# A 16 x 256 token RWKV and mixture-of-experts layer: earlier loads and norms, 22 idle products, a first table in PSUM, a tail on two queues

## What is computed

```python
x = x + attn(_layernorm(x), ...)
x = x + moe(_layernorm(x), ...)

# attn
xn = _ln(x, ln1_g, ln1_b); xp = _shift(xn)
k = (xn * mix_k + xp * (1.0 - mix_k)) @ Wk          # v and r likewise
r = sigmoid(...)
# per feature, along the tokens: a = ew*a + exp(k)*v;  b = ew*b + exp(k);  wkv = a / (b + 1e-8)
x = x + r * wkv @ Wo
yn = _ln(x, ln2_g, ln2_b); yp = _shift(yn)
kk = square(relu((0.5 * yn + 0.5 * yp) @ Wfk))
return x + sigmoid(yn @ Wfr) * (kk @ Wfv)

# moe: 8 experts, the best 2 of each token, hidden size 256
total_probs = softmax of the top 2 of x @ gate_w, at their experts
hidden = silu(h1) * h2                               # h1, h2 = x @ w12 of each expert
y = sum over experts of total_probs * (hidden @ w3)
```

## Time and profile before

| | |
|---|---|
| Runs | 330.14, 330.01, 329.98 us; median 330.01 |
| Profiled execution | 332.63 us, span 330.8 us, mean granted clock 0.92 |
| PE busy | 260.2 us (79%) |
| DVE busy | 241.2 us (73%) |
| POOL busy | 212.0 us (64%) |
| ACT busy | 196.4 us (59%) |
| Moved | 29.23 MB, mean 88 GB/s |

### The profile page before, as it was taken

One profiled execution on the slowest core, in us unless ns is written; L12 is line 12 of the kernel. 1 busy time (PEld: TensorE's weight loads), 2 busy tenths in 40 slices (PEclk: granted clock), 3 DMA queues, 4 the chain that ended last, 5 costly groups with the idle time before them and its releaser, 6 DMA issues.

```text
span 330.8 us, 6269 instructions
## 1 busy us (share of the span) xinstructions
PE 260.2 (79%) x1684; PEld 206.3 (62%) x1684; DVE 241.2 (73%) x735; ACT 196.4 (59%) x412; POOL 212.0 (64%) x225
## 2 busy tenths in 40 slices
PE   0684869999979999794796899379998799999300
PEld 0231347485746758482385799279998799999200
DVE  3076799899979799799959656776666366666790
ACT  3554288798876887585387267226676467675000
POOL 5215147625786887978376676777777777766760
PEclk9997899999989999998599599879999999999855
DMA  7930000000011111111254011142522333336583
GB/s 264 425 114 0 1 0 2 32 3 33 32 65 34 33 40 42 48 39 61 58 130 106 33 54 60 43 121 67 137 82 71 93 106 96 93 95 204 197 290 129
DMA packets 22418, 29.23 MB, mean 88 GB/s; under 512 B 4317, under 2 KB 15583, under 8 KB 22128
## 3 DMA queue, kind: packets, MB, share of 16 engines
q1 hardware_dynamic: 14832, 13.45, 14.4%
q0 software_dynamic: 4352, 8.47, 7.7%
q10 hardware_dynamic: 3200, 6.90, 5.6%
HBM read 15.09 MB, written 12.14 MB: 82 GB/s over the span
## 4 chain that ended last, share of the span: by engine, by line
DVE 26%; PE 20%; POOL 14%; issue 14%; DMA 6%; SPq 2%; ACT 2%; POOLq 0%; DVEq 0%; ACTq 0%
POOL res_d L459 8%; PE p_up L839 7%; POOL rows_d L442 3%; DVE st L897 3%; PE p_up L746 2%; PE p_f L758 2%; DMA res_d<-yo,xg 2%; DVE p_up L959 2%; DMA o_raw<-res_d 2%; DVE num L952 2%; DVE full L1101 2%; DVE xm L1003 2%; DVE den L948 1%; DVE mv L904 1%; DVE early L1117 1%
## 5 line engine op out<-in xcount | busy, mean ns | idle before, releaser
L442 POOL DMA_INDIRECT rows_d<-rows,pos x64 | 65.5, 1024 | 22.4 <-issue 21.8
L839 PE MATMUL p_up<-xgT,w_up 128*128 128x128 f32 x576 | 73.2, 282 | 2.2 <-DVE hid L1131 1.8
L839 PEld LDWEIGHTS p_up<-xgT,w_up 128*128 128x128 f32 x576 | 69.8, 198 | 2.5 <-issue 2.5
L459 POOL DMA_INDIRECT res_d<-yo,xg x48 | 47.9, 997 | 17.9 <-issue 17.0
L1127 DVE SCALAR_TENSOR_TENSOR gate_h<-th,p_up 128x512 f32<-128x512 f32 x36 | 24.7, 687 | 37.4 <-ACT th L615 36.4
L635 ACT ACTIVATE w_up<-w_exp 128x512 f32 x72 | 41.3, 622 | 7.0 <-DVE slot_w L1111 4.3
L615 ACT ACTIVATE th<-p_up 128x512 f32<-128x512 f32 x36 | 21.5, 596 | 34.4 <-PE p_up L839 32.1
L746 PE MATMUL p_up<-ysum,w_sb 128*128 128x512 f32 x64 | 35.6, 656 | 2.4 <-POOL ysum L421 2.4
L758 PEld LDWEIGHTS p_f<-wfv_half,kk 128*128 128x128 f32 x256 | 30.8, 192 | 3.9 <-issue 3.3
L758 PE MATMUL p_f<-wfv_half,kk 128*128 128x128 f32 x256 | 32.2, 278 | 0.0
L704 PE MATMUL p_up<-xn,w_mix 128*128 128x512 f32 x32 | 20.1, 714 | 15.1 <-DVE rw L966 11.8
(11 more groups left out here) (167 smaller groups left out, 562.1 us busy)
## 6 DMA issues: line engine op xcount, KB each, us to landing
o_raw<-res_d SPq DMA_DIRECT2D x16, 256.0 KB, 5.5
xg<-rows_d SPq DMA_DIRECT2D x48, 65.0 KB, 1.9
w_exp<-experts ACTq DMA_DIRECT2D x1, 3072.0 KB, 16.9
x_all<-x SPq DMA_DIRECT2D x10, 256.0 KB, 2.3
out<-x_all ACTq DMA_DIRECT2D x8, 256.0 KB, 2.4
o_raw<-rows_d SPq DMA_DIRECT2D x24, 65.0 KB, 2.0
x_all<-x SPq DMA_DIRECT2D x1, 1536.0 KB, 16.7
rows_d<-rows,pos POOLq DMA_INDIRECT x64, 2.4
```

The lines of the kernel that those rows point to most:

```text
L442: pool.indirect_dma_start(out=rows_d[:, :], out_offset=bass.IndirectOffsetOnAxis(ap=row, axis=0), in_=rows_of[c % 2][:, t, k, :], in_offse ...
L459: pool.indirect_dma_start(out=res_d[:, :], out_offset=bass.IndirectOffsetOnAxis(ap=row, axis=0), in_=yo[b][:, n, :], in_offset=None, bound ...
L839: mm = pe.matmul(p_up[b][:, n, h * P:(h + 1) * P], w_up[q % 2][:, n, h * P:(h + 1) * P], xgT[q % 2][:, n, :], start=True, stop=True)
```

## The change

Five parts:

- **Loads.** The expert weights' load moves from ACT's queue, where it stood behind w_sb, to SP's, behind the loads of x.
- **Norms and banks.** The groups of the first norm become (0,1), (1,2), (2,4), (4,6) and (6,8). The first four are made ahead of the loop; the statistics of chunks 6 and 7 are made one per iteration, with lag 1, behind `invert`, and POOL's power for them has lag 3. The reciprocal of chunks 0 and 1 goes to the banks p_h[0] and p_h[1], which nothing else uses that early, and v_in of chunks 1 and 2 waits for ekv. ffn_in of chunk 0 in turn waits for rw.
- **Weights and idle products.** ACT scales Wk alone ahead of z1(0), Wv behind it, Wr and Wfv behind xn(0). PE's single warm-up product becomes 22 products of 128x128 of the identity with itself, ahead of the wait for the weights.
- **First table.** Its small operands lie in the bank of k, and `early_shares` is joined to it. `up(0)` waits for its 11 links.
- **Tail.** The even chunks of k = 1 are loaded by SP and the odd ones by ACT, each queue stores the other half, and DVE makes all 16 additions, interleaved.

```diff
+            return p_h[c] if c < 2 else p_v
...
-        LN1_GROUPS = [(0, 1), (1, 2), (2, 5), (5, CHUNKS)]
+        LN1_GROUPS = [(0, 1), (1, 2), (2, 4), (4, 6), (6, CHUNKS)]
...
+        def results_written(eng, engine, k):
+
+            written = [nc.values_load(last_scatter[0:1, k, u:u + 1], engines=(engine,), min_val=32,
+                                      max_val=32 * LATE_ROUNDS) for u in range(BUFS)]
+            for u in range(BUFS):
+                eng.wait_ge(S[f"scattered{u}"], written[u])
+
+        def load_results(eng, k, chunks):
+
+            res_v = res_d[k * TOKENS:(k + 1) * TOKENS, :].rearrange("(p t) d -> p t d", p=P)
+            for c in chunks:
+                eng.dma_start(o_all[:, k, tiles(c), :], res_v[:, tiles(c), :]).then_inc(S[f"o_in{k}_{c}"], 16)
+
+        def store_sums(eng, chunks):
+
+            for c in chunks:
+                eng.wait_ge(S["higher_added"], c + 1)
+                eng.dma_start(out[:, tiles(c), :], x_all[:, tiles(c), :]).then_inc(S["stored"], 16)
...
+            sp.dma_start(w_exp[:, :], experts_in).then_inc(S["experts_in"], 16)
...
+            results_written(sp, mybir.EngineType.SP, 0)
+            load_results(sp, 0, range(CHUNKS))
+            results_written(sp, mybir.EngineType.SP, 1)
+            load_results(sp, 1, range(0, CHUNKS, 2))
+            store_sums(sp, range(1, CHUNKS, 2))
+
+            for u in range(BUFS):
+                sp.wait_ge(S[f"scattered{u}"], 32 * LATE_ROUNDS)
...
-            pipeline(pool, [(add_ffn, 3), (shift_sum, 2), (add_residual, 2), (ln3_power, 3), (last_ln1_power, 2),
+            pipeline(pool, [(add_ffn, 3), (shift_sum, 2), (add_residual, 2), (ln3_power, 3), (last_ln1_power, 3),
                             (dispatch_first, 4), (ln2_power, 1), (dispatch_second, 4), (gate_sums, 0)], {(9, 4): [(scatter, 0)], (9, 5): [(scatter, 1)], (10, 0): [(scatter, 2)]})
 
             for q in range(3, PAIRS):
                 scatter(q)
-
-            pool.wait_ge(S["x3_kept"], 16 * CHUNKS)
-            for c in range(DVE_CHUNKS, CHUNKS):
-                add_result(pool, 0, c, "lower_added_pool")
-
-            for u in range(BUFS):
-                pool.wait_ge(S[f"scattered{u}"], 32 * LATE_ROUNDS)
 
...
-            act.dma_start(w_exp[:, :], experts_in).then_inc(S["experts_in"], 16)
...
+            def mix_weights(n):
+
+                w = W(("Wk", "Wv", "Wr")[n])
+                act.activation(w_mix[:, n, 0, :], w, ACT.Copy, scale=mix[:, n:n + 1])
+                act.activation(w_mix[:, n, 1, :], w, ACT.Copy, scale=rest_mix[:, n:n + 1]).then_inc(S["w_mixed"], 1)
+
+            def halve_weights(_):
+
+                act.activation(wfv_half[:, :], W("Wfv"), ACT.Copy, scale=0.5).then_inc(S["w_mixed"], 1)
+
+            mix_weights(0)
...
+                     {(0, 16): [(mix_weights, 1)], (1, 8): [(mix_weights, 2), (halve_weights, 0)],
+                      (9, 18): [(expert_weights, 0)], (10, 1): [(turned_rows, 0)],
...
-                act.wait_ge(S["higher_added"], c + 1)
-                act.dma_start(out[:, tiles(c), :], x_all[:, tiles(c), :]).then_inc(S["stored"], 16)
+            act.wait_ge(S["early_scattered"], 32 * EARLY_PAIRS)
+            act.wait_ge(S["table_used"], 1)
+            results_written(act, mybir.EngineType.Activation, 1)
+            load_results(act, 1, range(1, CHUNKS, 2))
+            store_sums(act, range(0, CHUNKS, 2))
...
             pe.wait_ge(S["ident_ready"], 1)
+            pe.wait_ge(S["consts"], 9)
+
+            def warm_up(products, unread):
+
+
+                for _ in range(products):
+                    pe.matmul(unread[:, 0:P], ident[:, :], ident[:, :], start=True, stop=True)
+
+            warm_up(22, p_f)
             pe.wait_ge(S["weights_in"], 16)
-
...
-            warm_up(1, p_f)
-
-            pe.wait_ge(S["w_mixed"], 4)
...
                     after(pe, "xn_ready", c + 1)
+                    if c == 0:
+                        pe.wait_ge(S["w_mixed"], n + 1)
...
-            v_in = project(1, p_v, "v_done", lambda c: [("rw_ready", c)])
+            v_in = project(1, p_v, "v_done", lambda c: [("ekv_ready" if c <= 2 else "rw_ready", c)])
...
+                    if c == 0 and f < 2:
+                        pe.wait_ge(S["rw_ready"], f + 1)
                     pe.matmul(p_h[f % 2][:, :], W("Wfk")[:, f * P:(f + 1) * P],
...
+                    pe.wait_ge(S["early_steps"], EARLY_LINKS)
                     pe.wait_ge(S["rw_ready"], CHUNKS)
...
-                    ln1_group(len(LN1_GROUPS) - 1)
+                first, last = LN1_GROUPS[-1]
+                if c < last - first:
+                    ln1(first + c)
 
...
-                early_link(dve.tensor_scalar(full[:, :], part[:, :], WHOLE, -WHOLE, ALU.add, ALU.add))
-                dve.tensor_tensor_scan(full_cum[:, :], ones_e[:, :], full[:, :], 0.0, ALU.mult, ALU.add)
-                early_link(dve.tensor_scalar(full_coef[:, :], full[:, :], -float(P), float(REGION), ALU.mult, ALU.add))
-                early_link(dve.tensor_tensor(past[:, 0:some, :], spread_e(slot_no[:, 0:some], some),
-                                             spread_s(full_cum[:, :], some), ALU.is_ge))
-                dve.tensor_tensor(past_rows[:, 0:some, :], past[:, 0:some, :], spread_s(full_coef[:, :], some), ALU.mult)
-                early_link(dve.tensor_reduce(slot_e[:, 0:some], past[:, 0:some, :], mybir.AxisListType.X, ALU.add))
-                early_link(dve.tensor_reduce(slot_first[:, 0:some], past_rows[:, 0:some, :], mybir.AxisListType.X, ALU.add))
+                counts, part, full, full_cum, coef = (p_k[:, n * E:(n + 1) * E] for n in range(5))
+                until, shares, steps = (p_k[:, n * E:(n + 1) * E] for n in range(5, 8))
+                first, expert = p_k[:, 64:64 + some], p_k[:, 64 + some:64 + 2 * some]
+                early_link(dve.tensor_scalar(part, counts, 1.0 / P, (1 - P) / (2.0 * P), ALU.mult, ALU.add))
+                early_link(dve.tensor_scalar(full, part, WHOLE, -WHOLE, ALU.add, ALU.add))
+                dve.tensor_tensor_scan(full_cum, ones_e[:, :], full, 0.0, ALU.mult, ALU.add)
+                early_link(dve.tensor_scalar(coef, full, -float(P), float(REGION), ALU.mult, ALU.add))
+                early_link(dve.tensor_tensor(past[:, 0:some, :], spread_e(slot_no[:, 0:some], some), spread_s(full_cum, some),
+                                             ALU.is_ge))
+                dve.tensor_scalar(early_cum[:, 1:E + 1], full_cum, float(EARLY_SLOTS), None, ALU.min)
+                dve.tensor_scalar(until, full_cum, float(EARLY_SLOTS), None, ALU.min)
+                early_link(dve.tensor_tensor(past_rows[:, 0:some, :], past[:, 0:some, :], spread_s(coef, some), ALU.mult))
+                early_link(dve.tensor_reduce(first, past_rows[:, 0:some, :], mybir.AxisListType.X, ALU.add))
                 dve.scalar_tensor_tensor(out=slot_row[:, 0:some], in0=slot_no[:, 0:some], scalar=float(P),
-                                         in1=slot_first[:, 0:some], op0=ALU.mult, op1=ALU.add).then_inc(S["early_row"], 1)
-                dve.tensor_scalar(slot_w[:, 0:some], slot_e[:, 0:some], float(E - 1), float(EW), ALU.min, ALU.mult)\
+                                         in1=first, op0=ALU.mult, op1=ALU.add).then_inc(S["early_row"], 1)
+                early_link(dve.tensor_reduce(expert, past[:, 0:some, :], mybir.AxisListType.X, ALU.add))
+                dve.tensor_scalar(slot_w[:, 0:some], expert, float(E - 1), float(EW), ALU.min, ALU.mult)\
                     .then_inc(S["early_w"], 1)
-
-            def early_shares(_):
-
-                early_link(dve.tensor_scalar(early_cum[:, 1:E + 1], full_cum[:, :], float(EARLY_SLOTS), None, ALU.min))
-                early_link(dve.tensor_tensor(early[:, 0:E], early_cum[:, 1:E + 1], early_cum[:, 0:E], ALU.subtract))
-                dve.tensor_tensor(step_coef[:, :], early[:, 1:E + 1], early[:, 0:E], ALU.subtract)
-                early_link(dve.tensor_scalar(late_base[:, :], slot_no[:, :], early[:, 0:1], None, ALU.add))
-                early_link(dve.tensor_scalar(step_coef[:, :], step_coef[:, :], float(P), float(REGION), ALU.mult, ALU.add))
+                early_link(dve.tensor_tensor(shares, until, early_cum[:, 0:E], ALU.subtract))
+                early_link(dve.tensor_copy(early[:, 0:E], shares))
+                dve.tensor_tensor(late_base[:, :], slot_no[:, :], shares[:, 0:1].to_broadcast([P, LATE_SLOTS]), ALU.add)
+                early_link(dve.tensor_tensor(steps, early[:, 1:E + 1], shares, ALU.subtract))
+                early_link(dve.tensor_scalar(step_coef[:, :], steps, float(P), float(REGION), ALU.mult, ALU.add))
...
+            def add_lower(c):
                 add_result(dve, 0, c, "lower_added")
-            for c in range(CHUNKS):
-                if c < DVE_CHUNKS:
-                    dve.wait_ge(S["lower_added"], c + 1)
-                else:
-                    dve.wait_ge(S["lower_added_pool"], c - DVE_CHUNKS + 1)
+
```

(4 more changed lines are left out.)

45 lines of the change are left out of this document (13 added, 32 removed).

## The result

| | before | after |
|---|---|---|
| median of the runs | 330.07 us (329.98 to 332.33, 4 runs) | 308.56 us (308.16 to 313.04, 4 runs) |
| ratio, 95% interval | | 0.9329 [0.9279, 0.9379] |
| profiled execution: time, span | 332.63, 330.8 us | 308.16, 306.4 us |

A forecast was written before the change was run, and what follows sets the result against it. It took the kernel as bound by a ramp of waits, a full chunk loop, and a chain through two small VectorE operations and GpSimd's transfers. 9.0 + 7.7 + 1.5 = 18.2 us off the median gave 311.8 us, range 307.5 to 318.0.

The forecast's parts named there:

- Head: Start up to the first ekv: x lands by about 11.7, first ekv at 18.1 where it was 23.21; 5.1 us.
- Ramp: First to fourth ekv: fourth at 54.4 against 63.38; 9.0 us with the head's 5.1 in it, bounds 7 and 11.
- 3.9 is nearer to the second: Ramp: TensorE's 3.9 us gap, nearer 4.91 than 2.49, taken to bring the low clock; ekv(2) at 38.7.
- held scans: Ramp: GpSimd's power for chunks 4 and 5 might hold the first scans on VectorE; ramp would gain 2.4 us less.
- First table: Small VectorE operations before the first expert product: PSUM operands end the stalls; 3.7 us, bounds 0 and 4.9.
- second stall: Operations behind ffn(6), L1117 among them, go; up(2) keeps the full clock; 7.7 us with the first table, bounds 4.5 and 8.5.
- Late pairs: Pairs behind the last dispatch: nothing changes, all hangs on the last dispatch; 0 us.
- Tail: Final additions and stores: VectorE's stall goes, but DMA is full save one hole worth 0.8 us; 1.5 us, bounds 0.5 and 3.
- the kinder clock: Rival: no clock drop before v(2), the rest at upper values, 11 + 8.5 + 2 = 21.5; 308.5 us, chance 0.14.
- The loop lost: Rival that the loop cannot use all the gain: ramp 7, tables 4.5, tail 0.5; 318.0 us, chance 0.18.
- x didn't go on sharing: Rival at the head: x keeps sharing with the weights and lands at 18.4; 318.5 us, chance 0.06.
- far from 37: Rival slower: TensorE drops to 1.2 GHz in the loop, deciding from 37 us at the low clock; 348, chance 0.02.

The follow-up runs named there:

- the table put back: Changed kernel with the first table as before: small tiles in SBUF, shares as five operations, up(0) behind one link; 317.60 us, ratio 0.9625.
- one operation in SBUF: Changed kernel plus one 128x8 multiplication by 1 between SBUF tiles in the middle of the first table; 312.93 us, ratio 0.9488.
- late memset: Changed kernel plus one 128x64 memset at the end of GpSimd's program, waiting for VectorE's eighth lower addition; 313.40 us, ratio 0.951.
- the second execution of before: Kernel before, unchanged, profiled once more: 330.06 us, span 328.3 us.
- one product: Changed kernel with 1 idle product of 128 columns in place of 22; 308.45 us, ratio 0.9358.

## Why the prediction was right, and where it wasn't

It was right in sign and size, 18.2 us forecast against 21.5 by the medians. By its own steps:

- **Head, 5.1:** 5.35 (first ekv at 17.86, forecast 18.1; x at 11.48, forecast 11.7). The order of the transfers alone is worth 6.7 in the changed kernel. The idle products ended at 11.17, ahead of the forecast 12.5; they weren't late. The forecast had 5.7 us for them at the full clock and 11.4 at the low one, from a merged row with its ends; by the single records it is 4.9 and 9.4. What I missed is how little hangs on them: about 1 us of the first ekv, and nothing that the time shows.
- **Ramp, 9.0 in all:** 10.8 to 11.6 at the fourth ekv, 10.5 to 10.9 at the eighth. The step that failed is "3.9 is nearer to the second, so I take turn_y(0) and v(2) at the low clock": the gap was 3.18 us and the clock stayed full. ekv(2) fell at 36.46, forecast 38.7. With "the clock kept it is 11" the text had the number. Two prices inside the term were off and made up for each other: the guard of v is worth 7 us, not 4, and the order of the norms 1 us at the fourth ekv and nothing of the time. The 2.4 us that the prediction weighed for held scans didn't come: the power of chunks 4 and 5 ran from 18.03 to 20.93 beside both scans of chunk 0 (18.46 and 20.05), and each took 1.22 us as before.
- **First table, 3.7:** from the eighth ekv to rw(7) it takes 144.35 - 127.64 = 16.7 us, where it took 158.76 - 138.52 = 20.2: 3.5. With the **second stall** 6.9 to 8.6 by the milestones, 8.5 by the table put back; forecast 7.7. The mechanism was right: the run with one operation in SBUF shows it for the first stall, and the rows of after for the second (the variance held, one gap, the full clock, no wait of GpSimd).
- **Late pairs, 0:** 0.8 to 1.0.
- **Tail, 1.5:** 3.6 to 3.9 in the profiles of the whole change, above my upper bound of 3, and by the times 4.1 for additions and closing waits moved on the kernel before and 6.5 for the whole tail there. The profile of after has the longest tail of its kind: eight profiles with this tail and no late memset, on the changed kernel, have 15.9 to 18.0 us, so 3.6 to 6.0 us are won. It is the largest miss, and of the reason. I read the earlier trace rows as a stall on VectorE and the earlier trace rows as the one hole, and costed the move of GpSimd's additions by what VectorE does. But the kernel ended with GpSimd's drain, which stood behind its closing waits, and moving these and the additions let it start earlier. A look at the stage table behind 326 would have shown an end in which nothing works and no data move.
- **Rivals:** the kinder clock, 308.5, is the case that came. That it meets the median to 0.1 us is luck: against the second execution of before its ramp, 11, and its tables, 8.5, are 0.5 and 1.6 too large, and late pairs and tail, 0 and 2, together 2.4 too small. The loop lost 0.3 to 0.7 us of the ramp's gain, not 2. x didn't go on sharing. In the profile TensorE was at the low clock for 3.6 us of the stage of the earlier trace rows, far from 37.

## What to carry to other kernels

Before you cost the last transfers of a kernel, ask what its last microseconds are made of: if neither DMA nor an engine works there, an engine's closing drain may, and GpSimd's, which ends some 9 us behind its last work or its last wait, is cheap to hide by giving both to another engine. A small VectorE operation that takes microseconds beside plain GpSimd operations is mended by an operand in PSUM, and one such operation on the path is enough to pay for the search. A guard in a chunk loop must be priced for each chunk in which it acts. The order of work on an engine that is busy throughout was worth next to nothing here.

## What the runs showed of the hardware that I had not expected

- GpSimd's DRAIN at the program's end lasts 9.21 us in both executions of before, though GpSimd had worked nothing for over 1 us when it started, and 9.39 beside the late memset, 9.23 behind its end. In the eleven profiles in which it starts beside the last indirect transfers it ends 9.22 us behind the last of them (six), or 4.62 us behind the landing of their data where that is later (five). VectorE's drain in after ends 0.05 us behind VectorE's last addition. The Trainium skill (Perfetto Trace Analysis, Sequencer-only Instruction) says that the profiled part of such an instruction excludes its semaphore wait, so this would be work of the drain itself or a wait for its engine. What it does there the trace doesn't show.
- TensorE came out of gaps of 2.49 (before, 43.43), 2.69 (one product, 35.00) and 3.18 us (after, 33.98) at the full clock and kept it, and out of one of 2.61 (late memset, 13.72) at the full clock but lost it before the next pair. The nine heads with 22 products say the same: 1.20 us kept the clock, 1.08 lost it. The length of a gap alone doesn't tell the clock behind it.
- Idle products of 128 columns in float32, two records each, come 0.43 us apart at 1.2 GHz and 0.22 at 2.4 (their records 0.21 and 0.11); 22 of them took 6.5 to 8.0 us in the nine profiles that have them, since the clock rose at different times.
